# Operand buffers at multiples of 64 bytes, and a written order for the feed-forward's first tile

## The reference

```python
x = x + attn(layernorm(x))       # latent attention, 16 heads of 32 + 16 rotary features,
                                 # scores clipped to +-80, causal mask, softmax, then W_O
x = x + ffn(layernorm(x))

def fp4_quant_dequant(x):        # per block of 16 values of the last dimension
    scale = max(max(abs(xb)) / 6.0, 1e-12)
    idx = searchsorted(MID, abs(xb / scale))        # round to 0, 0.5, 1, 1.5, 2, 3, 4 or 6
    return GRID[idx] * sign(xb / scale) * scale

def fp4_linear(x, w):            # both operands quantised and multiplied back
    return einsum('bsk,nk->bsn', fp4_quant_dequant(x), fp4_quant_dequant(w))

def ffn(x):                      # w_gate, w_up: 1408 x 512; w_down: 512 x 1408
    h = silu(fp4_linear(x, w_gate)) * fp4_linear(x, w_up)
    return fp4_linear(h, w_down)
```

## Time and profile before

| what | us |
|---|---|
| median of 3 runs (lowest to highest) | 3002.51 (3002.14 to 3005.1) |
| the profiled execution's own time | 3003.13 |
| its span in the profile | 3001.4 |
| PE busy, share of the span | 2925.5, 97% |
| DVE busy | 2684.1, 89% |
| ACT busy | 1589.5, 53% |
| POOL busy | 580.7, 19% |
| mean granted clock of PE, as a share of full speed | 0.993 |

### The profile page before, as it was taken

The page is one execution under the profiler, slowest core; times in us unless marked ns, Lnnn a source line. Parts: engine busy times, 40 slices in busy tenths (PEclk is TensorE's granted clock), DMA queues, the critical chain, the costliest instruction groups (busy, mean ns, idle before and its releaser), DMA issues.

```text
span 3001.4 us, 65378 instructions
## 1 busy us (share of the span) xinstructions
PE 2925.5 (97%) x22500; PEld 2134.2 (71%) x22500; DVE 2684.1 (89%) x4593; ACT 1589.5 (53%) x2330; POOL 580.7 (19%) x620
## 2 busy tenths in 40 slices
PE   7999899999999999969999999999999999999999
PEld 6777644444444444458888888888888888888887
DVE  7999788888888888869999999999999999999996
ACT  5666578778778778643333333333333333333333
POOL 3444300000000000012222222222222222222221
PEclk9999999999999999989999999999999999999999
DMA  7889956566566566441222222222222221221220
GB/s 241 283 288 301 285 126 148 131 147 143 133 150 137 137 151 135 130 127 54 58 60 60 60 60 59 51 58 58 59 60 60 59 59 54 56 58 57 59 57 30
DMA packets 335143, 333.27 MB, mean 111 GB/s; under 512 B 60368, under 2 KB 242512, under 8 KB 335056
## 3 DMA queue, kind: packets, MB, share of 16 engines
q1 hardware_dynamic: 335056, 332.26, 40.7%
HBM read 215.52 MB, written 116.65 MB: 111 GB/s over the span
## 4 chain that ended last, share of the span: by engine, by line
PE 56%; DVE 1%; ACT 0%; DMA 0%; POOL 0%; issue 0%; SPq 0%; DVEq 0%
PE p_ring L2010 21%; PE p_ring L2036 16%; PE ps_od L2010 12%; PE ps_od L1990 6%; PE p_ring L2024 1%; PE ps_od L2036 0%; PE p_ring L2052 0%; PE p_ring L2017 0%; DVE sb_wg_lo L1908 0%; PE p_ring L1990 0%; DMA sb_x<-in_L_attn_x_dram 0%; DVE sb_wd_lo L1908 0%; DMA dn<-sb_x_big 0%; DVE sb_x_amax L106 0%; DVE sb_x_big L118 0%
## 5 line engine op out<-in xcount | busy, mean ns | idle before, releaser
L1063 ACT ACTIVATE sb_probs<-scores 128x1024 f32<-128x1024 f32 (+3 forms) x512 | 405.8, 840 | 112.8 <-PE scores L1269 106.5
L1657 POOL TENSOR_TENSOR sb_stage<-sb_stage,sb_h_inv 128x512 f32<-128x512 f32 (+1 forms) x192 | 190.4, 992 | 866.6 <-DVE sb_h_inv L112 866.6
L2010 PE MATMUL p_ring<-sb_wg_hi,sb_xq_hi 128*128 128x512 f32 (+1 forms) x1024 | 294.8, 369 | 0.3 <-DVE sb_wd_lo L1908 0.3
L2010 PE MATMUL p_ring<-sb_wg_lo,sb_xq_hi 128*128 128x512 f32 (+1 forms) x1024 | 290.6, 365 | 0.0
L2010 PE MATMUL p_ring<-sb_wg_hi,sb_xq_lo 128*128 128x512 f32 (+1 forms) x1024 | 289.4, 363 | 0.0
L2036 PE MATMUL p_ring<-sb_wd_hi,sb_ht_hi 128*128 128x512 f32 x693 | 278.8, 402 | 0.0
L2036 PE MATMUL p_ring<-sb_wd_hi,sb_ht_lo 128*128 128x512 f32 x693 | 274.2, 396 | 0.0
L2036 PE MATMUL p_ring<-sb_wd_lo,sb_ht_hi 128*128 128x512 f32 x693 | 273.7, 395 | 0.0
L1269 PEld LDWEIGHTS scores<-sb_q_hi,sb_k_hi 32*128 32x128 f32 x1536 | 73.6, 182 | 280.7 <-ACT sb_probs L1063 156.6
L811 POOL TENSOR_TENSOR sb_at_in<-sb_at_in,sb_inv_in 128x512 f32<-128x512 f32 x64 | 95.0, 1484 | 910.4 <-DMA sb_inv_in<-dinv 910.1
L1727 ACT ACTIVATE sb_stage<-sb_stage,sb_code_zero 128x512 uint8<-128x512 f32 (+1 forms) x192 | 139.5, 727 | 241.8 <-DVE sb_stage L122 241.8
(11 more groups left out here) (215 smaller groups left out, 7202.4 us busy)
## 6 DMA issues: line engine op xcount, KB each, us to landing
kq<-sb_kq_out SPq DMA_DIRECT2D x32, 1024.0 KB, 7.2
sb_kq_raw<-kq SPq DMA_DIRECT2D x64, 512.0 KB, 6.9
sb_xin<-in_L_attn_x_dram SPq DMA_DIRECT2D x32, 512.0 KB, 6.9
v<-sb_v_out SPq DMA_DIRECT2D x64, 256.0 KB, 6.5
rq<-sb_r_out SPq DMA_DIRECT2D x64, 256.0 KB, 4.5
sb_qr<-rq SPq DMA_DIRECT2D x32, 512.0 KB
sb_kr_hi<-kr SPq DMA_DIRECT2D x32, 512.0 KB
sb_kr_lo<-kr SPq DMA_DIRECT2D x32, 512.0 KB
```

The source lines that it names most:

```text
L1063: act.activation(probs(k)[:, 2 * pair:2 * pair + 2, off:BANK], scores[(2 * k + pair) % RING2][:, :, off:BANK], ACT.Exp, scale=SCALE).then_ ...
L1657: pool.tensor_tensor(x, x, spread(h_inv[:, a // QB:b // QB], (b - a) // QB), ALU.mult).then_inc(h_y, 1)
L2010: i = pe.matmul(ps[:, m, 0:b0 - a0], xt[a][:, c, :], wg[b][:, m, c, a0:b0], start=(c == 0 and a == b == 0), stop=(c == DC - 1 and a == 1))
```

## The change

There are two parts.

**Addresses.** Buffers are allocated one behind the other in a partition, the `Front` ones from its upper end. A small buffer `edge` of 32 bytes is put first at the upper end, and several small buffers (row statistics, scales, `code_zero`) are moved behind the large ones. What that does to the addresses, in bytes from the start of a partition, modulo 64:

| buffers | used by | before | after |
|---|---|---|---|
| `xt_hi`, `xt_lo`, `c_hi`, `c_lo` | PE, projections | 32 | 0 |
| `rope`, `turned`, `turned_kr`, `piece_in`, `piece_y`, `piece_big`, `piece_tmp` | DVE, POOL | 32 | 0 |
| `kr_hi0`, `kr_lo0`, `qr0`, `v0` (set s = 0 only), `r_out`, `v_out` | PE, attention | 32 | 0 |
| `ht_hi`, `ht_lo` | PE, `down` | 32 | 0 |
| `wg_*`, `wd_*`, `wo_*`, `at_hi`, `at_lo`, `xq_hi`, `xq_lo`, `w_hi`, `w_lo`, `k_*`, `q_*`, set s = 1 | PE | 0 | 0 |
| `piece_amax`, `piece_inv`, `h_scale` | DVE | 0 | 32 |
| `x_amax`, `x_scale`, `x_inv`, `h_inv` | DVE | 32 | 0 |

No instruction is changed by this.

**The first tile.** ACT, DVE, PE, POOL and SP get an order of their own for the first body. `project`, `residual`, `normalise` and `x_to_y` of tile (0, 1) now stand among jobs 14 to 21; its `x_to_q` and `code_x` among jobs 24 to 26; `turn_x` ahead of gate slice 2 and no longer behind it. The x part of tile (0, 0) moves a few jobs forward. SP loads the rows of tile (0, 1) behind piece 14, and the attention output and the inverses of tile (0, 2) behind piece 23. POOL's division of tile (0, 2) and its `at_lo` part are done before the first body, and ACT's `round_attention(0, 2)` stands behind job 20. The stores of the attention's last results stand behind piece 8 and no longer behind piece 11. ACT runs one Silu on a single value behind job 3.

```diff
@@ -1337 +1339 @@
-UNITS3_FIRST = [u for u in UNITS3 if u not in ("HT0", "HT1", "DN")]
+UNITS3_FIRST = ["WO", "G0", "G1", "XT", "G2"]
@@ SP @@
-                if n == 18:
+                if n == 14:
+                    ahead.load_x(sp, 0, 1)
+                if n == 15:
                     store_x_scale(0, 0)
-                if n == 20:
+                if n == 17:
                     spread_x_scale(0, 0)
-                if n == 11:
+                if n == 23:
+                    sp.wait_ge(ps_free, number(0, -1, "WO") + RING3 + 1)
+                    ahead.load_tile(sp, 0, 2)
+                    sp.wait_ge(ahead.at_divided, 2)
+                    ahead.load_inverse(sp, 0, 2)
+                if n == 8:
                     sp.wait_ge(o_copied, 1)
...
@@ ACT, before the first body @@
+                if n == 3:
+                    act.activation(silu_ready[:], code_zero[:], ACT.Silu)
                 if n == 5:
                     round_attention(0, 1)
-                if n == 8:
+                if n == 6:
                     act.wait_ge(last_stored, 32)
                     normalise(0, 0)
...
+                if n == 18:
+                    normalise(0, 1)
                 if n == 20:
-                    round_x(0, 0, (0, -1))
+                    round_attention(0, 2)
+            def first_tile():
+                for n in range(GATE_JOBS, FIRST_LATE):
+                    round_job(n)
+                    if n == 22:
+                        magic_x(0, 1)
+                    if n == 26:
+                        code_x(0, 1)
+                silu_of(0, 0, 0)
+                for n in range(FIRST_LATE, len(jobs)):
+                    round_job(n)
+                    if n == 30:
+                        magic_h(0, 0, 0)
...
@@ DVE @@
+                if n == 14:
+                    residual(0, 1, (0, 0))
+                if n == 20:
+                    x_to_y(0, 1)
+            def first_tile():
+                for n in range(GATE_JOBS, FIRST_LATE):
+                    rest_of_job(n)
+                    if n == 24:
+                        x_to_q(0, 1)
+                hidden(0, 0, 0)
+                for n in range(FIRST_LATE, len(jobs)):
+                    rest_of_job(n)
+                    if n == 31:
+                        round_hidden(0, 0, 0)
+                hidden(0, 0, 1)
+                decode_x(0, 1, (0, 0))
+                round_hidden(0, 0, 1)
+                hidden(0, 0, 2)
+                rest_of_x(0, 1)
+                round_hidden(0, 0, 2)
...
@@ PE @@
+                if n == 14:
+                    project(0, 1, (0, 0))
             pe.wait_ge(lo, GATE_JOBS)
...
-                if following:
+                if following and not first:
                     project(q, r + 1, (q, r))
                 for s in range(3):
                     if s < 2 and exists(q, r - 1):
                         turn_hidden(q, r, s)
+                    if first and s == 2:
+                        turn_x(q, r + 1, (q, r))
                     gate_up(q, r, s)
```

More of the change, by code:

```diff
@@ L1661, in _ @@
             rest_of_attention(0, 1)
+            inverse_deviation(0, 1)
+            divide(0, 2)
+            rest_of_attention(0, 2)
             def body(q, r):
-                if exists(q, r + 1):
+                first = flags(q, r)[0]
+                if exists(q, r + 1) and not first:
                     inverse_deviation(q, r + 1)
                 hidden_y(q, r, 0)
-                if exists(q, r + 2):
+                if exists(q, r + 2) and not first:
                     divide(q, r + 2)
-                if flags(q, r)[0]:
+                if first:
                     pool.wait_ge(ps_ready, number(q, r, "G1") + 1)
@@ L1770, in body @@
                     round_hidden(q, r, 0)
-                if first:
-                    for n in range(GATE_JOBS, 25):
-                        round_job(n)
                 if following:
                     magic_x(q, r + 1)
-                if first:
-                    for n in range(25, FIRST_LATE):
-                        round_job(n)
                 silu_of(q, r, 0)
@@ L1781, in body @@
                     round_hidden(q, r, 1)
-                if first:
-                    for n in range(FIRST_LATE, len(jobs)):
-                        round_job(n)
-                        if n == 30:
-                            code_x(q, r + 1)
                 magic_h(q, r, 0)
-                if following and not first:
+                if following:
                     code_x(q, r + 1)
@@ L1799, in body @@
                 code_hidden(q, r, 1)
-                if first:
-                    act.wait_ge(constants, 4)
                 code_hidden(q, r, 2)
@@ L1930, in body @@
                     decode_hidden(q, r, 0)
-                if first:
-                    for n in range(GATE_JOBS, 24):
-                        rest_of_job(n)
                 if following:
@@ L1937, in body @@
                     rest_of_hidden(q, r - 1, 0)
-                if first:
-                    for n in range(24, FIRST_LATE):
-                        rest_of_job(n)
                 hidden(q, r, 0)
@@ L1943, in body @@
                     decode_hidden(q, r, 1)
-                if first:
-                    for n in range(FIRST_LATE, 30):
-                        rest_of_job(n)
                 if following:
                     x_to_q(q, r + 1)
-                if first:
-                    for n in range(30, len(jobs)):
-                        rest_of_job(n)
                 round_hidden(q, r, 0)
@@ L1964, in body @@
                     result(q, r - 1)
-                if first:
-                    dve.wait_ge(ahead.chunk_loaded, 16 * 2 * B)
-                    ahead.invert_chunk(dve)
             iterations(dve, body)
```

70 lines of the change are left out of this document (43 added, 27 removed).

## The result

| | median us | lowest to highest | runs |
|---|---|---|---|
| before | 3003.81 | 3002.14 to 3005.31 | 4 |
| after | 2983.48 | 2981.65 to 2985.09 | 4 |

The ratio is 0.9932, its 95% interval 0.9915 to 0.9949: 20.3 us less, where 19.9 were forecast. The profiled execution has a span of 2979.9 us, 21.5 less than the one of before. That the sum came out so well is partly luck: one of its four terms was nearly twice too large, others were too small, and 4.4 us came from two stretches for which nothing was forecast. This table cuts both spans at the same events; the numbers are differences between starts in the two traces.

What follows compares the result with a forecast made beforehand. PE was taken to bound the feed-forward's steady state, with DVE near, and DVE the projections. Terms 8.5 + 0.5 + 0.5 + 10.4 = 19.9 us off 3003.1 made 2983.2, then 2982.6, given as 2983; range 2971 to 2995.

Steps and rivals of the forecast that it cites:

- Addresses, `down`: Feed-forward's `down`: 33 matmuls each 5.5 ns faster, 0.18 us a tile, limited by DVE to 8.5 us; bounds 0 and 11.6.
- Attention: Attention's score rounds, set s = 0 only: faster matmuls from the new addresses, taken as 0.5 us; bounds 0 and 2.2.
- rival A: All matmuls: the address does nothing, only the order gains, total 2992 us; chance 0.11.
- Addresses, projections: Projections: PE's work falls 7.2 us but DVE sets the half block, so 0.5 us; bounds 0 and 7.2.
- Rival B: Projections: they follow PE, so 7.2 - 0.5 us more is gained, total 2976 us; chance 0.10.
- The first tile: First feed-forward tile: new order brings the next `residual` at 1338.7, not 1349.1, a gain of 10.4 us; bounds 3.0 and 14.6.
- step (a): First tile up to the first gates: they start at 1308.1, with a new wait of about 2.3 us for the inverses.
- Step (b): First tile, gates 0 and 1 with 12 pieces of 1.35 us: gate 1 ends at 1327.1, before at 1335.0.
- step (c): First tile's tail, from gate 1's end to the next `residual`: 11.6 us in place of 13.4, ending at 1338.7.
- C: Steady feed-forward tiles: DVE becomes the bound as one more L120 runs beside POOL, total 3043 us; chance 0.03.
- D: First tile: it gains only 3 us, by later inverses and another half-clock stretch, total 2990.6 us; chance 0.10.

Runs made afterwards that it cites:

- experiments 2 to 4: Kernel after with `ht` alone at 32 (2996.1 us) or 64 (2994.2 us); matmuls timed by themselves behind it; all left-side buffers moved up 32 bytes (2984.32 us).
- addr_only: Kernel before with the changed addresses alone, no instruction moved: 2991.03 us, ratio to before 0.9954.
- order_only: Kernel after with the old addresses, so the first tile's new order alone: 2994.79 us, ratio to before 0.9966.
- experiment 5: Kernel after, with new and with old addresses, one piece's quantisation per half block replaced by two small DVE copies: first attention scores 7.6 us apart.
- experiment 1: The change's two parts apart, against the kernel before: addresses alone 2991.03 us, the first tile's order alone 2994.79 us.
- experiment 4: Kernel after with every buffer of the partition's left side moved up 32 bytes, distances kept: 2984.32 us, ratio to before 0.9933.
- Experiment 6: Kernel after with tile (0, 2)'s loads behind piece 12, not 23: 2980.22 us; the same with `turn_x(0, 0)` two pieces later: 2981.03 us.
- the second block: Matmuls added behind the kernel after, 24 of each kind, both operands on one base modulo 256, offsets varied: 227 to 234 ns each.

## Why the prediction was right, and where it was not

**Addresses, `down`: the price right, the reason not, the size a little low.** 7.69 to 7.50 us is the 0.18 of the forecast. The reason given, that an operand at 32 modulo 64 costs 5.5 ns whichever it is, fell with experiments 2 to 4: the distance between the two operands modulo 256 decides. The rows on `down` and the projections could not tell the two apart, since in each slow pair one operand stood at 128 modulo 256 and the other at 160. Attention could have: in set s = 0 both rotary operands stood at 224 modulo 256, so at 32 modulo 64, and its groups were no slower than those of the other set. The forecast saw that and held it for rival A; it allowed up to 2.2 us here, and all groups but the first stayed within 0.03 us. `qr0` and the `kr` buffers stood 4096 and 8192 bytes apart before and do so now. Of PE's 11.6 us the forecast kept 8.5, because DVE's tile was put at 25.90. Measured are 25.87 and 10.2 us in the 61 tiles. DVE's slack was undersized: it gave at least 0.165 a tile, where 0.14 was taken. The forecast's own words, 0.085 of waiting and about as much again in overlap, make 0.17, and 0.17 x 61 = 10.4. The end gave 1.9 more; in the profiles with one part alone it gave 0.5 (`addr_only`) and 0.7 (`order_only`), so it is not the addresses' alone.

**Addresses, projections: right.** 0.9 us against 0.5, and experiment 5 shows the 7.6 us behind DVE. Rival B fell; rival A fell with experiment 1. By the rule that the forecast took from the Trainium skill ("SBUF — State Buffer", section "Specifications (TRN2)"), lines of 16 bytes, 0 and 32 modulo 64 are alike, and `down` would have kept its 7.69 us. For an operand by itself experiment 4 bears that out: all at 32 is as fast as all at 0. What the rule does not speak of is the distance between two operands, which costs 6.6 ns of 233.

**The first tile: 5.6 us, not 10.4.** This is the term that failed, step (a) above all. It put the gates 31.0 us behind `at_lo`; they came at 34.5. DVE's work up to there was right (25.7 us forecast, 25.1 measured), and so was the chain (inverses, division, `round_attention(0, 2)`, piece 21). Wrong was the idle time, put at 2.9 to 4 us and 2.3 for the inverses: it was 9.2. The step had no term for `project(0, 1)`, which it took at full clock and as ready when DVE comes to it. PE had waited for DVE and for x's codes, its clock had fallen, and `project(0, 1)`, moved into just this place, reached DVE 4.6 us after its start where tile (0, 0)'s took 3.0; DVE waited 2.85, the pieces stood still, and with them SP, which issued the rows ahead of the inverses 24.0 us behind `at_lo` where 21.9 had been estimated. The inverses then took 4.8 us to land behind their last issue (1299.69 to 1304.53) where 3.7 had been taken; that makes the rest of the delay. Step (b) was forecast at 19.0 us and took 19.5 up to the `silu` of gate 1, step (c) 12.3 and not 11.6. Experiment 6, with the inverses early and the clock back in time, has the gates 3.0 us and the residual 2.2 us sooner. How much of that is the inverses' was not taken apart. The other 2.6 us that were missing I did not get back.

The 5.6 is itself no firm number. 1.7 of it lies ahead of `residual(0, 0)`, which comes 5.6 us behind `at_lo` before, 3.9 in the kernel after, and 4.0 to 6.3 in the other profiles, of either order. From `residual(0, 0)` to `residual(0, 2)` the old order took 66.4 us before and 69.9 in `addr_only`; the new one took 62.5 in the kernel after, and 62.0 to 63.0 in the seven other profiles that have it unchanged, with the full work. So the order is worth 4 to 7 us there. The 9.4 of `order_only`, by the medians, includes what the other stretches gave. By each of these the term of 10.4 was too large.

**Luck.** 2.5 us of the profiled difference lie in the first group of the attention. In the profiles of this study that group takes 31.5 to 37.0 us, 32.6 and 35.6 in two kernels that differ in `ht` alone. In `addr_only` and `order_only` it takes 34.5 and 33.0. It is where PE first waits for the loads and ScalarE, and it scatters; nothing shows it to be part of the change. Nothing was forecast for it, nor for the end, where 1.9 us were gained. These 4.4 us stand in for most of the 4.8 by which the first tile fell short.

**Rivals C and D.** C did not come: the steady tile became shorter. But the forecast had counted its pairs wrongly. It took one L120 in a tile to stand beside POOL; in the trace of before there are two already, that of `xq` beside POOL's division (mean 1665 ns in all 58) and one of the three of `stage` beside `at_lo`, and in the kernel after the same two. D, a gain of only 3, was nearer to the truth for its own term than the forecast's size (5.6), and both of its reasons came in part: the inverses landed 3.3 us later than worked out, though not behind another set of issues, and the clock was at half once more.

## What to carry to other kernels

Put the buffers of the two operands of a float32r matmul (the type of the _hi and _lo operands) a multiple of 256 bytes apart. It costs no more than looking at the addresses, and was worth 13 us of 3004 here. Before you count a faster engine's gain, find who sets the stretch: the same 7 us were worth 0.9 while VectorE set it. And where a step is moved behind a pause of TensorE, work it out at half the clock as well: the same twelve matmuls took 4.4 us in one kernel, and 3.1 in another whose clock had just come back.

## What the hardware showed

The time of a float32r matmul of 512 columns depends on how far apart its two operands lie in a partition (moving minus stationary, modulo 256 bytes): 226.7 ns at 0, 227 at 240, 229 at 64, 233 at 32, 96, 128 and 192, and 229 where the stationary operand was 192 ahead, which is the same 64. Moved by less than 32 bytes, the place counts too: 230 ns with both 16 on at a distance of 192, 240 ns with the moving operand 4 on. After a change to a distance of 0 the first matmuls are slower before they settle (236, 233 and 231 ns, then 226.7, in L2166 of the second block). Plain float32 took 429 ns at every offset tried.

The Trainium skill says in "SBUF — State Buffer", section "Who interferes with whom", that PE never waits on anyone. For other engines no run here shows otherwise. The 6.6 ns are a cost that the place of PE's own two operands has; that its weight load and its moving operand get in each other's way would explain it, but no run here shows this, and which resource they would share was not tried.
